# Shared expert's weights split once and reloaded as halves; routed experts' down products one step later

## The chip, the cores and the metric

The kernel runs on one core of one Trainium2 chip. The metric is the device time of one execution in microseconds, the median of several. The engines are named as in the profile: PE (TensorE, matmuls), PEld (its weight loads), DVE (VectorE), ACT (ScalarE), POOL (GpSimd) and SP (SyncE). SP and POOL issue nearly all DMAs here, each from its own queue, in program order: a DMA whose wait is not met holds back every DMA that stands behind it in that queue.

## The reference

Four sequences of 1024 tokens of width 512 go through one layer of two halves:

```python
x = x + layernorm(attention(layernorm(x)))       # lightning attention: 16 heads of 32, chunks of 128, a decayed running state
x = x + layernorm(moe(layernorm(x)))

def moe(x):                                      # 4096 tokens x 512
    shared = (silu(x @ sh_gate_w.T) * (x @ sh_up_w.T)) @ sh_down_w.T        # inner width 1408, every token
    probs = softmax(x @ router_weight.T); top 2 of 8 experts, weights divided by their sum
    for e in range(8):
        gate, up = split(x @ gate_up_proj[e].T)                             # 352 wide each
        out += (silu(gate) * up @ down_proj[e].T) * combine[:, e]
    return out + sigmoid(x @ shared_gate_w.T) * shared
```

## The kernel before

**Precision.** A large product of float32 matrices is made of three passes of a shorter type, `fp32r`: each operand is split into a high half (`_hi`, a copy rounded by ACT) and a low half (`_lo`, the rest, subtracted by DVE), and PE forms hi·hi, hi·lo and lo·hi (function `three`, lines 752 to 754). So every weight has to be split by an ACT copy and a DVE subtraction before PE can use it.

**Tiles.** The 4096 tokens are 8 blocks of 512 (`a` in the attention, `f` in the shared expert). The shared expert's inner width is 11 tiles of 128 (`NT`), so there are 88 units `n = 11 f + t`. A unit has on PE a gate product (`GA n`, 12 matmuls), an up product (`UP n`, 12) and a down product (`DN n`, 12), on ACT the silu (`SI`) and the high half of the hidden values (`HH`), on DVE the product (`SI`) and the low half (`HL`). The weights of a unit arrive as two raw pieces of 384 KB (`raw 2n` and `raw 2n+1`, issued by SP into three buffers) and are split by `SPL n half`: three ACT copies and three DVE subtractions for a unit. This is done again for each of the 8 blocks, 88 times in all. `WGU` (2) and `WDN` (3) are the numbers of buffers of gate/up and of down halves.

**Order.** `schedule()` writes one list of pieces, and every engine runs its own pieces in the order of that list. The attention pieces of a block are placed by the numbers in `PLACES` (a period of 44 for a block); the parts of the shared expert (`ffn_parts`: a first part with `GA`, a second with `UP`, a third with `DN` of the unit before) are filled in between. Attention pieces that the text speaks of: `QK` (8 products that make q and k), `V`, `S` (scores; DVE then multiplies them with the decay mask into `probsT`), `IP` (needs that `probsT`), `ST` (state), `OUT` (output product), `T1` and `T2` (transposes), `L` (residual and layernorm, about 5 us on DVE). `wa` loads one of 16 tiles of the attention weights, already stored as halves, 2 x 256 KB; `xr` loads the residual, `xin` the next block's x, `xti f` the transposed x of block `f` for the shared expert (8 loads of 256 KB, chunk by chunk, as `UP` of the last unit of block `f-1` gives the chunks free).

**The three stages.** Up to about 1200 us attention and the shared expert are interleaved (units 0 to about 58). Then the shared expert runs alone to unit 76, and in units 66 to 68 DVE works out the experts' pages of tokens (`SP 0` to `SP 5`). From about 1400 to 1890 us come the routed experts: 39 groups of 256 tokens (every fifth, from group 4 on, has only one subtile), 71 subtiles of 128 tokens, called steps `j`. Last come the 11 units of the last block with the final normalisation.

**A step of the routed experts** (`moe_step(j)`). PE: `GU j k` for k = 0 to 3 (gate and up products, 24 matmuls of 352 columns in all), `HT` (transposes of the hidden values), `XT` (transposes of the x of the next step), `MD` (down product, 9 matmuls). ACT and DVE: `WG g k` and `WD g k` split the weights of group `g` (4 and 3 pieces), `XT` and `HT` halve what PE has transposed, `MS` makes the hidden values; ACT evicts the down product (`MD`). POOL issues, in the order of the list: `rgu g` and `rdn g` (load the raw weights; there is one buffer for the down weights, so `rdn g+1` waits until DVE has split the last piece of group `g`), `xg` (gathers tokens) and `yo j` (adds the result of step j to the output in DRAM; it waits for ACT's eviction and for the adds of the group before). ACT's `WD g 0` waits for the landing of `rdn g`, and everything behind it on ACT waits with it.

Of the kernel before, what the change touches and what calls it, by code (L numbers as in the profile page):

```python
# [16 lines left out]
P = 128  # L17
D = 512
# [69 lines left out]
    "KT": (18, 27.16, 35.35, 42.69,),
    "S": (19, 20, 22.82, 23.75, 27.43, 27.98, 30.89, 30.98, 34.99, 36.49, 38.49, 39.49, 43.69, 44.69, 46.69, 47.69,),
    "V": (21.15, 21.85, 23.3, 23.85,),  # L90
    "IP": (22.07, 24.69, 29.52, 32.07, 37.88, 40.58, 46.23, 48.78,),
    "ST": (25, 32.57, 41.49, 50.17,),
    "OUT": (28.97, 35.43, 43.94, 50.69,),
    "LO": (36.6, 51,),
    "LN": (37.92, 53.57,),
    "L": (38.45, 53.31,),
    "LX": (39.15, 54.8,),
    "x1o": (39.67, 41.23, 52.1, 54.3,),
    "T2": (41.6, 42.6, 56, 56.74,),
    "xto": (58.7,),  # L100
    "R1": (58,),
    "R2": (59.41,),
    "SM1": (59.42,),
    "SM2": (60.46,),
    "SM3": (61.11,),
    "SM4": (62.32,),
    "CM": (62.12,),
    "RK": (64.43,),
    "sc": (59.36,),
    "PG": (66.47,),  # L110
# [1572 lines left out]
```

## Time and profile before

| | us |
|---|---|
| median of 3 runs | 2010.15 (2004.2 to 2010.46) |
| the profiled execution, its own time | 2009.93 |
| its span | 2008.1 |
| PE busy, of the span | 1893.5 (94%) |
| PEld busy | 1533.8 (76%) |
| DVE busy | 1197.4 (60%) |
| ACT busy | 952.2 (47%) |
| POOL busy | 434.5 (22%) |
| moved by DMA | 387.67 MB, 193 GB/s on average |

A matmul of 512 columns is shown as 0.39 us long, but the next one starts 0.23 us after it: they are pipelined, and PE's pace is read from the starts. Idle time in brackets behind a row is what the engine waited before it, and for whom. Times of rows are counted from the start of the span.

### The profile page before, as it was taken

The page shows a single profiled execution, that of the slowest core. Times are in us where ns is not written, and L with a number is a line of the kernel's source. Part 1 is how long each engine was busy: PE and PEld are TensorE (multiplying, and loading weights), DVE is VectorE, ACT ScalarE, POOL GpSimd, SP SyncE. Part 2 cuts the span into 40 slices and gives each one's busy share as a digit, 9 for nine tenths or more (in the row PEclk, how much of TensorE's full clock was granted, in tenths as well). Part 3 has the DMA queues.
Part 4 walks back from the last instruction along what each step waited for, and adds up shares of the span by engine and source line. Part 5 has one row for each costly group of instructions (what it writes and reads, how often), then busy time and mean ns, then how long its engine had stood idle before and what let it go on. Part 6 is the DMA issues. An engine that isn't in the chain of part 4 may idle for free.

```text
span 2008.1 us, 27871 instructions
## 1 busy us (share of the span) xinstructions
PE 1893.5 (94%) x9880; PEld 1533.8 (76%) x9880; DVE 1197.4 (60%) x2788; ACT 952.2 (47%) x1916; POOL 434.5 (22%) x438
## 2 busy tenths in 40 slices
PE   7779999999999999999999999999899999999997
PEld 5566777777777776777777777778899988889875
...
GB/s 304 355 266 217 67 152 219 129 144 231 67 171 211 104 118 257 123 107 206 160 115 192 142 119 152 171 227 172 187 257 253 255 253 255 251 250 253 128 280 203
DMA packets 137705, 387.67 MB, mean 193 GB/s; under 512 B 16848, under 2 KB 16992, under 8 KB 130656
## 3 DMA queue, kind: packets, MB, share of 16 engines
...
q10 hardware_dynamic: 432, 0.07, 0.0%
...
## 4 chain that ended last, share of the span: by engine, by line
PE 73%; DVE 10%; DMA 8%; ACT 4%; issue 3%; SPq 1%; POOL 1%; ACTq 0%; DVEq 0%
PE banks L752 20%; PE banks L754 20%; PE banks L753 19%; DMA moe_dn_raw<-w_dn,w_index 5%; PE banks L819 4%; PE banks L833 2%; PE banks L839 2%; PE banks L826 1%; PE banks L785 1%; DMA x<-x 1%; PE banks L940 1%; DVE probsT L1309 1%; ACT moe_dn_hi L1083 1%; PE banks L946 1%; DMA ffn_w_raw<-w_ffn 1%
## 5 line engine op out<-in xcount | busy, mean ns | idle before, releaser
L752 PE MATMUL banks<-xT_hi,ffn_gate_up_hi 128*128 128x512 f32 x704 | 298.8, 424 | 8.5 <-DMA xT_lo<-xt_scratch 5.8
L754 PE MATMUL banks<-xT_hi,ffn_gate_up_lo 128*128 128x512 f32 x704 | 277.1, 394 | 0.0
L753 PE MATMUL banks<-xT_lo,ffn_gate_up_hi 128*128 128x512 f32 x704 | 276.4, 393 | 0.0
L752 PE MATMUL banks<-moe_gu_hi,moe_xT_hi 128*128 128x352 f32 x568 | 197.4, 348 | 6.5 <-DVE moe_xT_lo L1464 6.5
L1018 ACT COPY q_one_head<-qT 32x128 f32<-32x128 f32 x512 | 151.2, 295 | 87.5 <-PE banks L819 82.3
L1457 DVE TENSOR_TENSOR moe_gu_lo<-moe_gu_raw,moe_gu_hi 128x704 fp32r<-128x704 f32 x156 | 135.9, 888 | 89.0 <-ACT moe_gu_hi L1077 88.0
L754 PE MATMUL banks<-moe_gu_hi,moe_xT_lo 128*128 128x352 f32 x568 | 184.0, 324 | 0.0
L753 PE MATMUL banks<-moe_gu_lo,moe_xT_hi 128*128 128x352 f32 x568 | 183.2, 323 | 0.0
L752 PEld LDWEIGHTS banks<-xT_hi,ffn_gate_up_hi 128*128 128x128 f32 x704 | 133.4, 189 | 52.1 <-issue 10.8
L753 PEld LDWEIGHTS banks<-xT_lo,ffn_gate_up_hi 128*128 128x128 f32 x704 | 133.6, 190 | 33.5 <-issue 9.1
L754 PEld LDWEIGHTS banks<-xT_hi,ffn_gate_up_lo 128*128 128x128 f32 x704 | 133.1, 189 | 29.1
L657 POOL DMA_INDIRECT ffn_out<-moe_y,moe_x x71 | 115.9, 1633 | 170.4 <-ACT moe_y L1103 117.3
L1440 DVE TENSOR_TENSOR ffn_gate_up_lo<-ffn_w_raw,ffn_gate_up_hi 128x768 fp32r<-128x768 f32 (+1 forms) x176 | 120.8, 686 | 43.7 <-ACT ffn_gate_up_hi L1048 43.4
L1025 ACT CAST attT_hi<-banks 128x256 fp32r<-128x256 f32 x64 | 23.7, 371 | 253.3 <-PE banks L833 253.3
...
L752 PE MATMUL banks<-ffn_down_hi,hidden_hi 128*128 128x512 f32 x308 | 133.5, 433 | 6.1 <-DVE hidden_lo L1450 6.0
L819 PE MATMUL banks<-q_one_head,kT 128*128 128x512 f32 x256 | 132.9, 612 | 1.2 <-ACT q_one_head L1018 0.6
L1461 DVE TENSOR_TENSOR moe_dn_lo<-moe_dn_raw,moe_dn_hi 128x512 fp32r<-128x512 f32 x117 | 79.4, 689 | 87.1 <-ACT moe_dn_hi L1083 86.8
L754 PE MATMUL banks<-ffn_down_hi,hidden_lo 128*128 128x512 f32 x308 | 121.7, 395 | 0.0
L753 PE MATMUL banks<-ffn_down_lo,hidden_hi 128*128 128x512 f32 x308 | 121.1, 393 | 0.0
L1077 ACT CAST moe_gu_hi<-moe_gu_raw 128x704 fp32r<-128x704 f32 x156 | 119.0, 783 | 0.0
L605 POOL DMA_INDIRECT x_normed_by_expert<-x_normed,pos_int x64 | 65.1, 1018 | 248.3 <-DVE pos_int L1409 230.1
...
## 6 DMA issues: line engine op xcount, KB each, us to landing
ffn_w_raw<-w_ffn SPq DMA_DIRECT2D x176, 384.0 KB, 3.1
...
```

Of the source, the lines that this page charges most:

```text
L605: pool.indirect_dma_start(out=xs_d[:, :], out_offset=bass.IndirectOffsetOnAxis(ap=posi[:, NC * a + c, k:k + 1], axis=0), in_=xn2[:, c, :], ...
L657: pool.indirect_dma_start(out=acc_d[:, :], out_offset=bass.IndirectOffsetOnAxis(ap=xg[:, j % XG, D + 1:DX].bitcast(I32), axis=0), in_=y[:, ...
L752: pe.matmul(out_ap, l_hi, r_hi, start=start, stop=False)
L753: pe.matmul(out_ap, l_hi, r_lo, start=False, stop=False)
L754: return pe.matmul(out_ap, l_lo, r_hi, start=False, stop=stop)
L819: mm = pe.matmul(b, kT[:, g, c * P:(c + 1) * P], qz[:, g % 2].rearrange("p h t -> p (h t)"), start=True, stop=True)
L833: mm = pe.matmul(b[r, cols], v[:, c, g * P + j * HD:g * P + (j + 1) * HD], probs[:, g % 2, j, :], start=False, stop=(gl == 1), skip_group_ ...
L1018: op = act.copy(qz[r, g % 2, j, :], qT[r, g, c * P:(c + 1) * P])
L1077: op = act.copy(gu_hi[:, i % 2, k, :], rgu[:, i % 2, k * GU:(k + 1) * GU])
L1440: op = ve.tensor_tensor(wgu_lo[:, n % WGU, gu_cut], src, wgu_hi[:, n % WGU, gu_cut].bitcast(F32), ALU.subtract)
L1457: op = ve.tensor_tensor(gu_lo[:, i % 2, k, :], rgu[:, i % 2, k * GU:(k + 1) * GU], gu_hi[:, i % 2, k, :].bitcast(F32), ALU.subtract)
L1461: op = ve.tensor_tensor(dn_lo[:, i % 2, k, :], rdn[:, k * D:(k + 1) * D], dn_hi[:, i % 2, k, :].bitcast(F32), ALU.subtract)
```

## The change

1. **Weights stored as halves.** In block 0 the weights of the shared expert are loaded raw and split as before. After each split SP stores the halves in DRAM (`wst n`: 1024 KB of gate/up, 512 KB of down). For units 11 to 76 there is no `raw` and no `SPL`; SP loads the halves instead: `wl n 0` (gate and up, 1024 KB, placed behind `UP n-2`, for whose buffer it waits) and `wl n 1` (down, 512 KB, behind `DN n-3`). Units 77 to 87, after the experts, load raw and split as before. The high and low halves of a buffer now lie side by side, so that one DMA fills both.
2. **`xti` moved.** It stands right behind `UP` of the last unit of a block, no longer ahead of the next block's first unit.
3. **A step of the routed experts in another order.** `MD` and `yo` come a step later (of step j-2, behind `GU j 0`), `XT` stands ahead of `GU j 1`, `HT` behind it.
4. **Places moved.** `PLACES` shifts as a whole by 0.07 (some by 0.03 or 0.17); `xin` comes 0.45 earlier, the first `xr` 0.71 earlier, `CM` 0.37 earlier. A few pieces change places with a neighbour through this.

```diff
 def ffn_parts(n):
...
-    if n + 1 < NF:
-        first.insert(0, ("SPL", n + 1, 0))
-        second.insert(0, ("SPL", n + 1, 1))
-        for half in range(2):
-            u = 2 * (n + 1) + half + RAW
-            if u < 2 * NF:
-                (first, second)[half].insert(1, ("raw", u))
+    for half, part in enumerate((first, second)):
+        u = 2 * (n + 1) + half + RAW
+        if u < 2 * NT or 2 * F_MOE <= u < 2 * NF:
+            part.insert(0, ("raw", u))
+        if split_here(n + 1):
+            part.insert(0, ("SPL", n + 1, half))
+    if n + 1 < NT:
+        second.insert(1, ("wst", n + 1))
     if n % F_MOE:
         third += ffn_down(n - 1)
-    if t == 0 and n != F_MOE:
-        if f:
-            first.insert(0, ("xti", f))
+    if t == NT - 1 and n + 1 < F_MOE:
+        second.append(("xti", f + 1))
+    if NT <= n + WGU < F_MOE:
+        second.append(("wl", n + WGU, 0))
+    if NT <= n + WDN - 1 < F_MOE:
+        third.append(("wl", n + WDN - 1, 1))
...
     if live:
         out += [("GU", j, 0)]
-    if j:
-        out += [("HT", j - 1)]
+    if j >= 2:
+        out += [("MD", j - 2), ("yo", j - 2)]
+        if j >= 4 and j - 4 + XG < NJ:
+            out += [("xg", j - 4 + XG)]
     split()
+    if j + 1 < NJ:
+        out += [("XT", j + 1)]
     if live:
         out += [("GU", j, 1)]
-        if j + 1 < NJ:
-            out += [("XT", j + 1)]
     split()
+    if 1 <= j <= NJ:
+        out += [("HT", j - 1)]
     if live:
         out += [("GU", j, 2), ("GU", j, 3), ("MS", j)]
-    if j:
-        out += [("MD", j - 1), ("yo", j - 1)]
-        if j >= 3 and j - 3 + XG < NJ:
-            out += [("xg", j - 3 + XG)]
...
+            elif kind == "wst":
+                n, = args
+                sp.wait_ge(v_piece, done("V", "SPL", n, 1))
+                sp.dma_start(out=wfg_d[n], in_=wgu[:, n % WGU].rearrange("p i n -> p (i n)").bitcast(F32)).then_inc(wsplit_out[n % 4], 16)
+                sp.dma_start(out=wfd_d[n], in_=wdn[:, n % WDN].rearrange("p i n -> p (i n)").bitcast(F32)).then_inc(wsplit_out[n % 4], 16)
+            elif kind == "wl":
+                n, down = args
+                ring = WDN if down else WGU
+                sp.wait_ge(*split_stored(n % NT))
+                if n - ring < NT:
+                    sp.wait_ge(*split_stored(n - ring))
+                sp.wait_ge(p_piece, done("P", "DN" if down else "UP", n - ring))
+                dst, part, landed = (wdn, wfd_d, wdn_in) if down else (wgu, wfg_d, wgu_in)
+                sp.dma_start(out=dst[:, n % ring].rearrange("p i n -> p (i n)").bitcast(F32), in_=part[n % NT]).then_inc(landed[n % ring], 16)
...
             if kind in ("GA", "UP"):
                 if kind == "GA":
-                    pe.wait_ge(v_piece, done("V", "SPL", n, 1))
+                    if split_here(n):
+                        pe.wait_ge(v_piece, done("V", "SPL", n, 1))
+                    else:
+                        pe.wait_ge(wgu_in[n % WGU], 16 * ((n - NT) // WGU + 1))
...
                 act.wait_ge(raw_in[u % RAW], 16 * (u // RAW + 1))
                 if n >= WGU:
                     act.wait_ge(p_piece, done("P", "UP", n - WGU))
+                if WGU <= n < NT:
+                    act.wait_ge(*split_stored(n - WGU))
```

SP's queue before block 2 of the shared expert, before the change. `x1` is the residual of attention block 3 (`xr 3 2` and `xr 3 3`), `ffn_w_raw` are the raw weights of units 18 to 23, `xT_hi` and `xT_lo` the first chunk of `xti 2`:

```order
L714 DMA ffn_w_raw<-w_ffn 128x768 [waits dve_piece] x9
L689 DMA x1<-x 128x512 [waits act_piece,x1_out0]
L689 DMA x1<-x 128x512 [waits act_piece,x1_out1]
L724 DMA xT_hi<-xt_scratch 128x512 [waits xT_used,xT_out]
L724 DMA xT_lo<-xt_scratch 128x512
```

The same place after it (the loads of the halves of unit 22, `xti 2`, then the halves of unit 23):

```order
L750 DMA ffn_gate_up_hi_lo<-ffn_gate_up_split 128x2048 [waits pe_piece,ffn_w_split_out0]
L750 DMA ffn_down_hi_lo<-ffn_down_split 128x1024 [waits pe_piece,ffn_w_split_out0]
L768 DMA xT_hi<-xt_scratch 128x512 [waits xT_used,xT_out]
L768 DMA xT_lo<-xt_scratch 128x512
...
L750 DMA ffn_gate_up_hi_lo<-ffn_gate_up_split 128x2048 [waits pe_piece,ffn_w_split_out1]
L750 DMA ffn_down_hi_lo<-ffn_down_split 128x1024 [waits pe_piece,ffn_w_split_out1]
L718 DMA x1<-x 128x512 [waits act_piece,x1_out0]
L718 DMA x1<-x 128x512 [waits act_piece,x1_out1]
```

The loads of x no longer stand behind the residual's, and the weights wait for PE (`pe_piece`) instead of DVE.

POOL's queue where the routed experts begin, before the change: two stores of the shared expert's last block, `rgu 3`, two more stores, `yo 0` (with the waits for those stores), `rdn 2`, `yo 1`:

```order
L616 DMA ffn_out<-shared_staged 128x512 [waits act_piece] x2
L636 DMA moe_gu_raw<-w_gu,w_index 128x2816 [waits dve_piece]
L616 DMA ffn_out<-shared_staged 128x512 [waits act_piece] x2
L657 DMA ffn_out<-moe_y,moe_x 4352x512 [waits shared_out0,shared_out1,ffn_out_zero,act_piece]
L643 DMA moe_dn_raw<-w_dn,w_index 128x1536 [waits dve_piece]
L657 DMA ffn_out<-moe_y,moe_x 4352x512 [waits act_piece]
```

The same place after it:

```order
L641 DMA ffn_out<-shared_staged 128x512 [waits act_piece] x2
L661 DMA moe_gu_raw<-w_gu,w_index 128x2816 [waits dve_piece]
L641 DMA ffn_out<-shared_staged 128x512 [waits act_piece] x2
L668 DMA moe_dn_raw<-w_dn,w_index 128x1536 [waits dve_piece]
L682 DMA ffn_out<-moe_y,moe_x 4352x512 [waits shared_out0,shared_out1,ffn_out_zero,act_piece]
L661 DMA moe_gu_raw<-w_gu,w_index 128x2816 [waits dve_piece]
```

`rdn 2` now stands ahead of `yo 0`, so that only DVE's last split of group 1 holds it.

ACT in step 20 of the routed experts (`moe_dn_hi` are the pieces `WD 11 0` to `WD 11 2`, the first of which needs the landing of `rdn 11`), before the change:

```order
L1083 CAST moe_dn_hi<-moe_dn_raw 128x512 [waits pe_piece,moe_dn_in]
L1093 CAST moe_hT_hi<-banks 128x384 [waits pe_piece]
L1083 CAST moe_dn_hi<-moe_dn_raw 128x512 [waits pe_piece,moe_dn_in]
L1088 CAST moe_xT_hi<-banks 128x512 [waits pe_piece]
L1083 CAST moe_dn_hi<-moe_dn_raw 128x512 [waits pe_piece,moe_dn_in]
L1098 ACTIVATE moe_silu<-banks 128x352 [waits dve_piece,pe_piece]
L1103 ACTIVATE moe_y<-banks,moe_x 128x512 [waits moe_y_added0,pe_piece]
```

And after it:

```order
L1134 CAST moe_dn_hi<-moe_dn_raw 128x512 [waits pe_piece,moe_dn_in]
L1154 ACTIVATE moe_y<-banks,moe_x 128x512 [waits moe_y_added1,pe_piece]
L1134 CAST moe_dn_hi<-moe_dn_raw 128x512 [waits pe_piece,moe_dn_in]
L1139 CAST moe_xT_hi<-banks 128x512 [waits pe_piece]
L1134 CAST moe_dn_hi<-moe_dn_raw 128x512 [waits pe_piece,moe_dn_in]
L1144 CAST moe_hT_hi<-banks 128x384 [waits pe_piece]
L1149 ACTIVATE moe_silu<-banks 128x352 [waits dve_piece,pe_piece]
```

`moe_hT_hi`, which PE's `MD` needs, has moved from directly behind the first of these splits to a place behind all three, and the `MD` that uses it to the step after.

## Rows read from the trace of the kernel before

**Rows 1.** The page: busy time of each engine over the span.

```profile
PE 1893.5 (94%) x9880; PEld 1533.8 (76%) x9880; DVE 1197.4 (60%) x2788; ACT 952.2 (47%) x1916; POOL 434.5 (22%) x438
```

**Rows 2.** Windows by stage: us, busy by engine, PEclk, DMA share, GB/s.

```profile
0.00:200.00 200.00, 160.12 (x785) 118.60 (x786) 106.61 (x291) 81.21 (x188) 38.11 (x57) 0.92 0.84 286
200.00:1200.00 1000.00, 969.44 (x5039) 741.86 (x5038) 593.75 (x1582) 432.14 (x958) 78.67 (x108) 1.00 0.45 152
1440.00:1890.00 450.00, 436.84 (x2588) 404.02 (x2587) 288.64 (x444) 284.52 (x509) 245.48 (x196) 1.00 0.88 245
```

**Rows 3.** Waits of PE, 200 to 1200 us: total, times, longest.

```profile
PE banks L826 <- DVE probsT L1309: 5.5, 8, 0.9
PE banks L752 <- DMA xT_lo<-xt_scratch: 3.0, 6, 1.0
PE banks L752 <- DVE probsT L1309: 2.6, 7, 0.4
```

**Rows 4.** Waits of PE, 1320 to 1890 us.

```profile
PE banks L752 <- DVE moe_hT_lo L1466: 7.9, 7, 1.7
PE banks L752 <- DVE moe_xT_lo L1464: 6.5, 3, 5.5
PE banks L946 <- DVE moe_hidden L1470: 4.6, 5, 1.2
```

**Rows 5.** Groups by line: what splits the shared expert's weights.

```profile
L1440 DVE TENSOR_TENSOR ffn_gate_up_lo<-ffn_w_raw,ffn_gate_up_hi 128x768 fp32r<-128x768 f32 (+1 forms) x176 | 120.8, 686 | 43.7 <-ACT ffn_gate_up_hi L1048 43.4
L1437 DVE TENSOR_TENSOR ffn_down_lo<-ffn_w_raw,ffn_down_hi 128x512 fp32r<-128x512 f32 x88 | 60.6, 688 | 38.1 <-ACT ffn_down_hi L1046 36.7
```

**Rows 6.** Timeline of PE before and at `GA 22`: start, length, form, idle before.

```profile
549.77 0.39 PE L753 MATMUL banks<-xT_lo,ffn_gate_up_hi 128*128 128x512 f32 x1
550.00 0.39 PE L754 MATMUL banks<-xT_hi,ffn_gate_up_lo 128*128 128x512 f32 x1
...
559.59 1.02 PE L819 MATMUL banks<-q_one_head,kT 128*128 128x512 f32 x2
...
564.90 0.49 PE L752 MATMUL banks<-xT_hi,ffn_gate_up_hi 128*128 128x512 f32 x1 [0.35 <-DMA xT_lo<-xt_scratch]
```

**Rows 7.** Timeline of SP, 549 to 562 us.

```profile
552.74 0.85 SPq L689 DMA_DIRECT2D x<-x  x2
553.68 0.39 SPq L724 DMA_DIRECT2D xT_hi<-xt_scratch  x1
```

**Rows 8.** DVE on the raw shared weights, 1292 to 1317 us; then PE at `DN 66`.

```profile
1292.00:1317.00 25.00, 2.92 (x4) 0.93 0.48 152
...
1317.27 0.51 PE L752 MATMUL banks<-ffn_down_hi,hidden_hi 128*128 128x512 f32 x1 [4.11 <-DVE hidden_lo L1450]
```

**Rows 9.** Timeline of DVE, POOL and ACT, 1412 to 1429 us.

```profile
1412.44 0.69 DVE L1461 TENSOR_TENSOR moe_dn_lo<-moe_dn_raw,moe_dn_hi 128x512 fp32r<-128x512 f32 x1 [2.28 <-ACT moe_dn_hi L1083]
...
1420.37 1.51 POOL L643 DMA_INDIRECT moe_dn_raw<-w_dn,w_index  x1 [0.30 <-DVE moe_gu_lo L1457]
...
1428.04 0.62 ACT L1083 CAST moe_dn_hi<-moe_dn_raw 128x512 fp32r<-128x512 f32 x1 [7.72 <-DMA moe_dn_raw<-w_dn,w_index]
```

**Rows 10.** Windows, 1427.5 to 1434.4 us; columns as in Rows 2.

```profile
1427.50:1434.40 6.90, 4.32 (x16) 4.20 (x17) 3.93 (x7) 4.22 (x8) 2.91 (x3) 0.51 0.74 231
```

**Rows 11.** Timeline of POOL, 1536 to 1546 us, and of ACT and PE there.

```profile
1538.39 0.94 POOL L643 DMA_INDIRECT moe_dn_raw<-w_dn,w_index  x1 [0.30 <-DVE moe_gu_lo L1457]
...
1544.79 0.62 ACT L1083 CAST moe_dn_hi<-moe_dn_raw 128x512 fp32r<-128x512 f32 x1 [2.54 <-DMA moe_dn_raw<-w_dn,w_index]
...
1546.66 0.50 PE L752 MATMUL banks<-moe_dn_hi,moe_hT_hi 128*128 128x512 f32 x1 [1.18 <-DVE moe_hT_lo L1466]
```

**Rows 12.** DMA issues, whole span: count, KB each, median us to landing.

```profile
ffn_w_raw<-w_ffn SPq DMA_DIRECT2D x176, 384.0 KB, 3.1
xt_scratch<-xT_staged_lo POOLq DMA_DIRECT2D x7, 1024.0 KB, 8.2
```

**Rows 13.** The loads that touch `att_w_lo`, 200 to 1200 us.

```profile
DMA to landing us min/median/max: 2.8/4.5/9.1
```

More of the change, by code:

```diff
@@ L88 @@
[L88 to L110, printed above, removed]
+    "N1": (3.48, 4.07, 5.52, 6.52,),
+    "T1": (5.62, 6.95, 7.62, 8.62,),
+    "wa": (7.25, 7.43, 7.61, 7.79, 10.52, 10.08, 12.52, 13.52, 14.17, 15.52, 16.52, 18.84, 23.22, 23.37, 23.52, 23.27,),
+    "QK": (9.66, 11.07, 12.07, 13.22, 14.07, 15.07, 16.07, 16.78,),
+    "xr": (23.12, 24.37, 44.52, 44.74,),
@@ new lines @@
+    "Z": (16.39, 18.62, 20.77, 21.47, 25.5, 26.5, 28.65, 29.05, 33.66, 33.97, 36.82, 37.52, 42.06, 43.54, 44.99, 45.76,),
+    "KT": (18.17, 27.23, 35.38, 42.76,),
+    "S": (19.17, 20.07, 22.99, 23.92, 27.5, 28.05, 30.96, 31.05, 35.02, 36.52, 38.52, 39.52, 43.76, 44.76, 46.76, 47.76,),
+    "V": (21.22, 21.92, 23.37, 23.92,),
+    "IP": (22.24, 24.86, 29.59, 32.14, 37.91, 40.61, 46.3, 48.85,),
+    "ST": (25.17, 32.64, 41.52, 50.24,),
+    "OUT": (29.14, 35.5, 43.97, 50.76,),
+    "LO": (36.67, 51.07,),
@@ L111 @@
+    "LN": (37.99, 53.64,),
+    "L": (38.52, 53.38,),
+    "LX": (39.22, 54.87,),
+    "x1o": (39.74, 41.3, 52.17, 54.37,),
+    "T2": (41.67, 42.67, 56.07, 56.81,),
+    "xto": (58.77,),
+    "R1": (58.07,),
+    "R2": (59.48,),
+    "SM1": (59.49,),
+    "SM2": (60.53,),
+    "SM3": (61.18,),
+    "SM4": (62.39,),
+    "CM": (61.75,),
+    "RK": (64.5,),
+    "sc": (59.43,),
+    "PG": (66.54,),
     "W": (),
@@ L149, in attention_offsets, with split_here, raw_turn, raw_unit @@
     return s
+def split_here(n):
+    return n < NT or F_MOE <= n < NF
+def raw_turn(u):
+    return u if u < 2 * NT else u - 2 * (F_MOE - NT)
+def raw_unit(turn):
+    return turn if turn < 2 * NT else turn + 2 * (F_MOE - NT)
 def ffn_parts(n):
@@ L303, in schedule @@
     cut = ends.index(("EV", BEFORE - 1, 2))
-    start, tail = moe_step(0), moe_step(NJ)
+    start = moe_step(0)
     seq += ends[:2] + start[:1] + ends[2:cut] + [("xti", BEFORE)] + start[1:] + ends[cut:]
@@ L308, in schedule @@
     after = [part for n in range(F_MOE, NF) for part in ffn_parts(n)]
-    seq += tail[:1] + after[0] + tail[1:]
+    seq += moe_step(NJ) + after[0] + moe_step(NJ + 1)
     after[0] = []
@@ L418, in build @@
         raw = sb("ffn_w_raw", [RAW, UNIT])
-        wgu_hi = sb("ffn_gate_up_hi", [WGU, 2 * D], F32R)
-        wgu_lo = sb("ffn_gate_up_lo", [WGU, 2 * D], F32R)
-        wdn_hi = sb("ffn_down_hi", [WDN, D], F32R)
-        wdn_lo = sb("ffn_down_lo", [WDN, D], F32R)
+        wgu = sb("ffn_gate_up_hi_lo", [WGU, 2, 2 * D], F32R)
+        wdn = sb("ffn_down_hi_lo", [WDN, 2, D], F32R)
+        wgu_hi, wgu_lo = (wgu[:, :, i, :] for i in range(2))
+        wdn_hi, wdn_lo = (wdn[:, :, i, :] for i in range(2))
         shs = sb("shared_staged", [2, D])
@@ L555, in build @@
         sh_out = [sem(f"shared_out{i}") for i in range(2)]
+        wsplit_out = [sem(f"ffn_w_split_out{i}") for i in range(4)]
+        wgu_in = [sem(f"ffn_gate_up_in{i}") for i in range(WGU)]
+        wdn_in = [sem(f"ffn_down_in{i}") for i in range(WDN)]
         raw_in = [sem(f"raw_in{i}") for i in range(RAW)]
@@ L712, in sp_piece @@
                 else:
-                    sp.wait_ge(v_piece, done("V", "SPL", *divmod(u - RAW, 2)))
-                sp.dma_start(out=raw[:, u % RAW, :], in_=w_ffn[u // 2 % NT, u % 2]).then_inc(raw_in[u % RAW], 16)
+                    sp.wait_ge(v_piece, done("V", "SPL", *divmod(raw_unit(i - RAW), 2)))
+                sp.dma_start(out=raw[:, i % RAW, :], in_=w_ffn[u // 2 % NT, u % 2]).then_inc(raw_in[i % RAW], 16)
             elif kind == "xti":
@@ L899, in pe_ffn @@
                 pe.wait_ge(v_piece, done("V", "HL", n))
+                if not split_here(n):
+                    pe.wait_ge(wdn_in[n % WDN], 16 * ((n - NT) // WDN + 1))
                 if n == F_MOE:
@@ L1037, in act_ffn @@
                 half, = args
-                u = 2 * n + half
+                u = raw_turn(2 * n + half)
                 act.wait_ge(raw_in[u % RAW], 16 * (u // RAW + 1))
@@ L1432, in dve_ffn @@
                 half, = args
-                src = raw[:, (2 * n + half) % RAW, :]
+                src = raw[:, raw_turn(2 * n + half) % RAW, :]
                 ve.wait_ge(a_piece, done("A", kind, n, half))
```

14 lines of the change are left out of this document (7 added, 7 removed), and 2 rows, old and new, of the table PARTS.

## The prediction

> **What bounds the kernel now.** I read the page first, then the windows by stage, then the waits of PE in each stage, and last the timeline around the waits that stand out. PE is busy for 1893.5 us of 2008.1 [rows 1], no other engine for more than 60% except PE's own weight loads. The number of matmuls is not touched by the change, so its worth can only be PE's waits, some 115 us at most, and the lowered clock that follows long ones. By stage [rows 2]: the opening (to 200 us) leaves 40 us idle with the DMA engines 84% busy; the interleaved stage leaves 31 us of 1000; the routed experts, 1440 to 1890 us, leave 13 of 450. The reader is to see in the windows how thin PE's losses are spread: a gain has to be collected from many small places, and each must be a place that this change touches.
>
> **The splits that go.** DVE spends 120.8 + 60.6 us on 88 units [rows 5], 2.06 us each; 66 units lose them, 136 us of DVE work, and ACT loses the three copies ahead of them. Almost all of it lies beside PE's matmuls and is worth nothing by itself. It is worth something where PE waits for a DVE result that stands behind a split. In the interleaved stage PE waits for `probsT` in two rows, 5.5 + 2.6 us in 15 waits [rows 3]. Some of these are behind `L`, which stays, some behind a split. Evictions of banks that DVE does late are not all in these rows. Bounds: 0, if DVE's queue is held by what stays, and 13 us, if the 8.1 us go and as much again as half of that in the unlisted ones. I take 6, nearer the middle, because the waits are many and short and a split is 0.4 to 0.95 us long.
>
> **DVE's chain in the page stage.** From 1292 to 1317 us DVE works nearly without a pause on the pages, and `DN 66` starts at 1317.27 after 4.11 us of waiting for `hidden_lo`. Four subtractions of raw shared weights stand in that stretch, 2.92 us together [rows 8], and they go. PE gets just that, since DVE sets this place; whatever PE saves a few us earlier (its x for block 6 arrives sooner too) is waited for here. Gain 2.9; bounds 0, if ACT's evictions ahead of `HH 66` set it next, and 4.1, the whole wait.
>
> **`xti` earlier.** `GA 22` waits chunk by chunk. The last of its four chunks starts at 564.90. At the pace of undisturbed matmuls, 550.00 - 549.77 = 0.23, it would start 11 matmuls (two of scores, nine of `GA`) after 559.59, at 562.1 [rows 6]: 2.8 us lost, of which I leave 0.3 to the start of another product. SP issues the residual's loads at 552.74 and only then the first of xT at 553.68 [rows 7], though `UP 21` was running at 549.77 and gave the first chunk free within its first three matmuls. Now `xti 2` stands ahead of the residual and, for block 3, ahead of all that it followed. `GA 33` loses the same. PE's recorded waits for these are 3.0 us in 6 [rows 3]; the rest is loads landing between matmuls. Gain 5, bounds 3 and 6.
>
> **Start of the routed experts.** `rdn 2` was issued at 1420.37 behind `yo 0`; ACT took its data at 1428.04 after 7.72 us idle [rows 9], `XT 4` stood behind that, and PE waited 5.5 us [rows 4]. Then the granted clock was 0.51 for 6.9 us [rows 10]; PE worked 4.3 us in it, at half pace, which costs another 2.2. In the new order `rdn 2` needs only DVE's last split of group 1, which runs at 1412.44 for 0.69 [rows 9], so the data lands 1413.1 + (1428.04 - 1420.37) = 1420.8, before PE asks for `GU 4 0`. Gain 7, of 7.7; bounds 3 (it is slower, behind `rgu 3` in the queue) and 7.7.
>
> **Routed experts, steady.** PE waits 7.9 us for `moe_hT_lo` and 4.6 us for `moe_hidden`, 12 waits [rows 4]. One of them: `rdn 11` is issued at 1538.39 behind a `yo` and an `xg`; ACT takes it at 1544.79 after 2.54 us; the high half of hT stands behind, and PE's `MD` starts 1.18 us late, at 1546.66 [rows 11]. Now `HT` has three quarters of a step and `MD` a step more, `rdn` stands ahead of the `yo` that held it in this place, and between ACT's stall and PE's need lie GU products of about 1.1 us each. What is late next: `XT`, also behind the splits on ACT, for which PE leaves two GU, one `HT` and one GU, 3.5 us, where it had 4.3 (`MD` was among them). Halving takes 1.5, so ACT may be 2 us late before PE sees it, and it was 2.54 late here. Gain 10 of 12.5; bounds 3 and 12.5. The DMAs of `yo` only shift.
>
> **What it adds.** 66 units load 1536 KB for 768: 52 MB more, and 11 stores of 1536 KB, 17 MB. Nothing in the trace is a 1024 KB load on SP; the nearest rows are 1024 KB stores with 8.2 us to landing for the second of two, and 3.1 us for 384 KB [rows 12]. Even 8.2 is hidden: from `UP n-2` to `GA n` PE has at least `DN`, `GA`, `UP`, `DN`, 48 matmuls of 0.23 or 11 us. `wl` waits for PE, so SP can run less far ahead; but between the release of each attention tile and its use stands the same PE work as before, at least 24 matmuls and three transposes, some 6.7 us (tile 0 of a block); for tile 11 it is 7.6, for tile 4 8.2. Those loads take 4.5 us in the middle and 9.1 at most [rows 13]. The 16 engines are 45% busy in this stage at 152 GB/s [rows 2]; 69 MB more over some 1150 us is 60 GB/s more, which makes it some 63%. Cost: none, if the median holds; if tiles 0, 4 and 11 of six blocks all took 9.1 us, 2.4 + 0.9 + 1.5 = 4.8 us a block, 29 us. I take 3, near the median. The Trainium skill, page "DMA: Bandwidth & Descriptors", section "Issuing engines are not separate DMA queues", says that DMAs of all issuers run on the same 16 engines and interleave; by that the stores and loads would slow the attention's loads and POOL's too, and the sum would move toward the 29 us. No row here shows the added load; the trace's own 9.1 us agrees that loads in a crowd take twice as long.
>
> The stores add a wait on ACT (`SPL n` for the store of `n-2`), which holds copies and with them PE. The tightest is unit 2: between the end of split 0 and split 2 lie about `GA 0` and `UP 0`, 24 matmuls or 5.5 us, and a store of 1024 KB may take 8.2 [rows 12], 2.7 us more. I take 0, for a store alone in its queue lands sooner, and 3 us either way for the opening, the places moved included; their swaps of neighbours change nothing else that I can price.
>
> **Sum.** 6 + 2.9 + 5 + 7 + 10 = 30.9, less 3, is 28 us. The profiled execution took 2009.9 (span 2008.1 and 1.8 around it), the median of the runs is 2010.15; so 2010 - 28 = **1982 us**. All upper bounds: 13 + 4 + 6 + 7.7 + 12.5 + 3 = 46, 1964. All lower ones without the traffic: 0 + 0 + 3 + 3 + 3 = 9, 2001.
>
> **Rivals.**
> - *The waits among the experts move on to `XT` and the `yo` queue.* Their DMA engines are 88% busy [rows 2], so the landing of `rdn` is set by traffic, not by its place; ACT is as late as before and now holds `XT`. For it: slack of `XT` shrinks by 0.8 us. Against it: POOL was what delayed `rdn` in [rows 11]. The experts then give 3 + 2 instead of 17: 28 - 12 = 16 us, 1994.
> - *DVE and ACT work was hidden anyway and the traffic takes the rest.* The interleaved stage gives 0 instead of 6 and the traffic takes 20 instead of 3: 28 - 23 = 5 us, 2005; with all 29 of it, 2014. For it: the splits' waits are short ones; against it: no unit of the load is late by the count of PE work above.
> - *Slower: the attention's weights come late.* Place: `QK 0`, `QK 4` and `V 0` of each block. It decides once their landing passes 6.7 us; every us beyond costs up to 3 x 6 = 18 us. At 9.1 us it costs 29 instead of 3, which leaves 2 of the gain, 2008; two us beyond that another 36, which makes 2044. For it: the traffic of this stage grows by 40%. Against it: only one `wl` at a time is in flight and those tiles are issued after attention products, when the last `wl` has mostly landed.
>
> **How the numbers follow.** The forecast case, 15 to 44 us faster, 0.70; the first rival 0.14; the second 0.08; slower 0.06; better than all bounds 0.02. A measurement of this kernel tells 0.3% (6 us) from no change. Faster: 0.70 + 0.14 + 0.02 = 0.86; within, 0.08; slower, 0.06. The range takes the first two cases, 1965 to 2001, and leaves 0.16 out.
>
> **What would show it.** In the changed profile: `ffn_w_raw` about 44 loads instead of 176 and DVE about 1060 us busy; no wait for `xT_lo` at blocks 2 and 3; `DN 66` still waiting for DVE; no half clock where the experts begin; waits for `moe_hT_lo` and `moe_hidden` gone and at most 3 us for `moe_xT_lo`; the stage 200 to 1200 shorter by some 8 us with DMA at about 0.6. I am wrong if PE waits for `att_w`, `ffn_gate_up_hi_lo` or a store, or if the expert stage is not shorter by 10 us or more.

## The result and the profile after

The changed kernel takes 1996.7 us (median of 16 runs, 1985.8 to 2004.3) against 2008.1 us for the kernel before (16 runs, 2004.1 to 2013.8). The ratio is 0.9941, with a 95% interval of 0.993 to 0.9952: 0.6% or 11 us faster, inside the range, but not half of the 28 us forecast. The profiled execution took 2002.2 us, its span 2000.4, so the two profiles differ by 7.7 us, and the account below is of these.

Between the starts of certain pieces on PE (first matmul of each, from PE's timeline) the two profiled executions took, in us:

| stretch on PE | before | after | gained | forecast |
|---|---|---|---|---|
| start to `GA 2` | 196.7 | 193.3 | 3.4 | 0 |
| `GA 2` to `GA 55` | 998.2 | 996.9 | 1.3 | 8 (6 + 5 - 3) |
| `GA 55` to `GU 0 0` | 200.8 | 196.2 | 4.6 | 2.9 |
| `GU 0 0` to `GU 5 0` | 43.1 | 33.2 | 9.9 | 7 |
| `GU 5 0` to `GU 70 0` | 452.8 | 461.8 | -9.0 | 10 |
| `GU 70 0` to `UP 87` | 95.9 | 98.4 | -2.5 | 0 |

The forecast fails in two rows: the interleaved stage, and above all the routed experts, where a gain of 10 became a loss of 9. The stretch to `GU 0 0` gained more than its upper bound of 4.1.

The page of the changed kernel, busy time [rows 1]:

```profile
PE 1895.7 (95%) x9880; PEld 1536.0 (77%) x9880; DVE 1083.5 (54%) x2590; ACT 844.6 (42%) x1718; POOL 439.6 (22%) x438
```

DVE has lost 114 us and ACT 108, PE's work is the same. The windows by stage [rows 2, 10]:

```profile
0.00:200.00 200.00, 163.24 (x808) 120.82 (x812) 107.32 (x292) 81.12 (x188) 38.10 (x57) 0.93 0.88 311
200.00:1200.00 1000.00, 971.82 (x5043) 744.92 (x5036) 513.62 (x1445) 361.51 (x822) 78.94 (x109) 0.99 0.56 201
1400.00:1440.00 40.00, 39.91 (x238) 36.77 (x236) 24.41 (x38) 24.27 (x44) 17.02 (x14) 1.00 0.75 220
1440.00:1890.00 450.00, 433.60 (x2529) 398.92 (x2530) 282.72 (x431) 272.56 (x493) 247.43 (x191) 0.99 0.84 239
```

Where the experts begin (1400 to 1440) PE is busy throughout at full clock; the half clock of [rows 10] is gone. After it, PE is busy for 3 us less than before. PE's waits from 200 to 1200 us [rows 3]:

```profile
PE banks L796 <- DMA att_w_lo<-att_w_split: 6.7, 1, 6.7
...
PE banks L796 <- DVE probsT L1360: 2.3, 7, 0.3
PE banks L870 <- DVE probsT L1360: 2.1, 7, 0.9
```

The waits for `probsT` fell from 8.1 to 4.4 us and those for `xT_lo` are gone, as forecast; in their place stands one wait that is new. The waits among the experts, 1320 to 1880 us [rows 4]:

```profile
PE banks L796 <- DVE moe_hT_lo L1517: 12.5, 7, 2.9
PE banks L796 <- DVE moe_xT_lo L1515: 4.1, 6, 1.2
```

`moe_hidden` and the 5.5 us for `moe_xT_lo` are gone; `moe_hT_lo` has grown from 7.9 to 12.5 us in the same number of waits. Both new losses, seen close. First SP and PE around `QK 5 6`, timeline:

```profile
748.58 0.38 SPq L768 DMA_DIRECT2D xT_hi<-xt_scratch  x1
...
753.34 0.59 SPq L768 DMA_DIRECT2D xT_lo<-xt_scratch  x1
754.03 0.67 SPq L750 DMA_DIRECT2D ffn_gate_up_hi_lo<-ffn_gate_up_split  x1
754.75 0.66 SPq L731 DMA_DIRECT2D att_w_hi<-att_w_split  x1
755.44 0.49 SPq L731 DMA_DIRECT2D att_w_lo<-att_w_split  x1
...
769.51 0.77 PE L796 MATMUL banks<-x_normedT_hi,att_w_hi 128*128 128x512 f32 x1 [6.69 <-DMA att_w_lo<-att_w_split]
```

The weights of `QK 5 6` (`wa 5 6`) are issued behind the eight loads of `xti 3` and the 1024 KB of `wl 34 0`, and land 14 us later. PE then waits 6.69 us and starts its next matmuls 0.43 us apart instead of 0.23: the granted clock has fallen to half (1.2 GHz) within that wait, at 764.8 us, and stays there for 10 us. The windows of this place and of the first of three such places among the experts:

```profile
764.80:775.00 10.20, 5.49 (x13) 4.36 (x14) 3.08 (x18) 0.00 (x0) 0.00 (x0) 0.50 0.63 239
1495.00:1499.00 4.00, 4.00 (x16) 3.35 (x15) 0.90 (x3) 1.63 (x3) 1.60 (x2) 0.57 0.86 317
```

Second, step 23 of the experts, timeline of POOL, ACT and PE:

```profile
1547.15 1.62 POOL L682 DMA_INDIRECT ffn_out<-moe_y,moe_x  x1 [3.01 <-ACT moe_y L1154]
1549.08 1.23 POOL L646 DMA_INDIRECT moe_x<-x_normed_by_expert,x_index  x1 [0.30 <-issue]
1550.61 1.34 POOL L668 DMA_INDIRECT moe_dn_raw<-w_dn,w_index  x1 [0.30 <-DVE moe_hidden L1521]
...
1556.76 0.62 ACT L1134 CAST moe_dn_hi<-moe_dn_raw 128x512 fp32r<-128x512 f32 x1 [2.54 <-DMA moe_dn_raw<-w_dn,w_index]
1557.28 0.47 ACT L1144 CAST moe_hT_hi<-banks 128x384 fp32r<-128x384 f32 x1
...
1558.62 0.50 PE L796 MATMUL banks<-moe_dn_hi,moe_hT_hi 128*128 128x512 f32 x1 [1.66 <-DVE moe_hT_lo L1517]
```

`rdn 13` stands behind `yo 20`, which waited 3.01 us for ACT's eviction, and an `xg`; it lands 6.1 us after its issue, ACT stops 2.54 us for it, `HT 22` stands right behind that stop, and `MD 22` starts 1.66 us late. This repeats at `MD 13`, 22, 31, 40, 49 and 58, once in nine steps. The 9.0 us are accounted for by the window of the whole stretch in each kernel (before, then after):

```profile
1438.80:1891.60 452.80, 439.64 (x2602) 406.47 (x2601) 289.17 (x445) 285.65 (x510) 245.49 (x196) 1.00 0.87 244
```

```profile
1419.60:1881.40 461.80, 445.31 (x2603) 409.81 (x2602) 293.65 (x447) 282.82 (x510) 256.39 (x198) 0.99 0.84 241
```

Of the 9.0 us, 461.8 - 445.3 = 16.5 against 13.2, so 3.3, are more idle time, and 5.7 are matmuls that took longer, nearly all of it in the three periods of half clock.

### The profile page after: what moved, and what is told of

It is laid out like the page before. It is cut to its first block, busy times and chain, and to the rows that moved or that the text cites. A ratio compares the mean times of both kernels' runs of the same rounds, so it can differ in the third digit from the quotient of the medians.

```text
span 2000.4 us, 27565 instructions
## 1 busy us (share of the span) xinstructions
PE 1895.7 (95%) x9880; PEld 1536.0 (77%) x9880; DVE 1083.5 (54%) x2590; ACT 844.6 (42%) x1718; POOL 439.6 (22%) x438
## 4 chain that ended last, share of the span: by engine, by line
PE 56%; DMA 5%; DVE 5%; ACT 2%; issue 1%; POOL 1%; SPq 1%; ACTq 0%; DVEq 0%
PE banks L796 16%; PE banks L798 16%; PE banks L797 16%; DMA moe_dn_raw<-w_dn,w_index 3%; PE banks L863 2%; PE banks L989 1%; DMA ffn_w_raw<-w_ffn 1%; PE banks L877 1%; PE banks L995 1%; PE banks L883 1%; PE banks L870 1%; DMA att_w_lo<-att_w_split 1%; PE banks L829 1%; ACT moe_dn_hi L1134 0%; DVE fin_stats L1535 0%
## 5 line engine op out<-in xcount | busy, mean ns | idle before, releaser
L796 PE MATMUL banks<-xT_hi,ffn_gate_up_hi_lo 128*128 128x512 f32 x704 | 296.7, 422 | 9.8 <-DMA xT_lo<-xt_scratch 3.3
L798 PE MATMUL banks<-xT_hi,ffn_gate_up_hi_lo 128*128 128x512 f32 x704 | 276.8, 393 | 0.0
L797 PE MATMUL banks<-xT_lo,ffn_gate_up_hi_lo 128*128 128x512 f32 x704 | 276.1, 392 | 0.0
L796 PEld LDWEIGHTS banks<-xT_hi,ffn_gate_up_hi_lo 128*128 128x128 f32 x704 | 133.1, 189 | 49.2 <-issue 10.2
L797 PEld LDWEIGHTS banks<-xT_lo,ffn_gate_up_hi_lo 128*128 128x128 f32 x704 | 133.2, 189 | 33.9 <-issue 8.9
L798 PEld LDWEIGHTS banks<-xT_hi,ffn_gate_up_hi_lo 128*128 128x128 f32 x704 | 132.9, 189 | 29.0
L682 POOL DMA_INDIRECT ffn_out<-moe_y,moe_x x71 | 120.7, 1699 | 143.0 <-ACT moe_y L1154 63.1
L796 PE MATMUL banks<-ffn_down_hi_lo,hidden_hi 128*128 128x512 f32 x308 | 131.2, 426 | 2.3 <-DVE hidden_lo L1501 2.3
L1498 DVE TENSOR_TENSOR hidden<-banks,hidden 128x512 f32<-128x512 f32 x77 | 53.2, 691 | 129.2 <-PE banks L798 100.3
L796 PE MATMUL banks<-x_normedT_hi,att_w_hi 128*128 128x512 f32 x256 | 106.5, 416 | 17.6 <-DVE x_normedT_lo L1339 6.9
L1360 DVE TENSOR_TENSOR probsT<-banks,decay_mask 128x512 f32<-128x512 f32 x128 | 88.1, 689 | 63.7 <-PE banks L863 61.1
L798 PE MATMUL banks<-ffn_down_hi_lo,hidden_lo 128*128 128x512 f32 x308 | 120.8, 392 | 0.0
L797 PE MATMUL banks<-ffn_down_hi_lo,hidden_hi 128*128 128x512 f32 x308 | 120.2, 390 | 0.0
```

Of the source, the lines that this page charges most:

```text
L682: pool.indirect_dma_start(out=acc_d[:, :], out_offset=bass.IndirectOffsetOnAxis(ap=xg[:, j % XG, D + 1:DX].bitcast(I32), axis=0), in_=y[:, ...
L796: pe.matmul(out_ap, l_hi, r_hi, start=start, stop=False)
L797: pe.matmul(out_ap, l_hi, r_lo, start=False, stop=False)
L798: return pe.matmul(out_ap, l_lo, r_hi, start=False, stop=stop)
L1360: op = ve.tensor_tensor(probs[:, g % 2, :, :], chunked(b), mask[:, GH * g:GH * (g + 1), :], ALU.mult)
L1498: op = ve.tensor_tensor(hid[:, :], up_ps, sg[:, :], ALU.mult)
```

## The experiments

Twelve kernels, each timed against the kernel before and looked at in one profile. They were timed in three lots: experiment 1 and the first kernels of 2 and 3; the second kernels of 2 and 3 and the first of 4 and 6; the rest. The kernel before had medians of 2009.7, 2016.1 and 2009.1 us in them, so kernels of different lots are compared by their ratios. `GU 5 0` to `GU 70 0` is called the expert stretch.

**1. The old order of a step in the changed kernel, and the new order alone.** Two theories: A, the new order loses the 9 us; B, the halves' traffic or something earlier does.

```diff
     if live:
         out += [("GU", j, 0)]
-    if j >= 2:
-        out += [("MD", j - 2), ("yo", j - 2)]
...
+    if j:
+        out += [("HT", j - 1)]
     split()
-    if j + 1 < NJ:
-        out += [("XT", j + 1)]
     if live:
         out += [("GU", j, 1)]
+        if j + 1 < NJ:
+            out += [("XT", j + 1)]
     split()
-    if 1 <= j <= NJ:
-        out += [("HT", j - 1)]
     if live:
         out += [("GU", j, 2), ("GU", j, 3), ("MS", j)]
+    if j:
+        out += [("MD", j - 1), ("yo", j - 1)]
```

That is the first kernel's edit; the second makes the same edit the other way round in the kernel before.

> The changed kernel with the old order of an expert step (MD of the last step at its end, HT behind GU 0, rdn as before); all else as changed. Theory A (the new order itself costs the experts time): from GU 5 to GU 70 the old 453 us come back instead of 462, no half clock in that stage, MD's waits for moe_hT_lo no longer than 1.8 us; the 5.5 us wait where the experts begin comes back too, with its half clock, some 7 to 9 us. Total within 4 us of the changed kernel, 1993 to 2001. Rival B (the experts are slower for another reason: the weights' halves and their traffic, or the clock after the earlier stages): that stretch stays at 460 or more and the total is 2003 or more.

> The kernel before with only the new order of an expert step. Theory A: GU 5 to GU 70 takes 460 to 463 us instead of 453, with waits of MD for moe_hT_lo of 1.5 to 3 us and periods of half clock; the wait at GU 4 0 is gone (7 to 9 us won), so the total is within 4 us of the kernel before. Rival B: the stretch takes 443 to 453 us as it was forecast, and the total is 8 to 17 us below the kernel before.

Measured: 1995.6 us, ratio 0.993 (0.9911 to 0.9949), and 2009.5 us, ratio 0.9997 (0.9982 to 1.0012). The expert stretch of the first, then of the second, with PE's waits in it:

```profile
1426.40:1877.40 451.00, 439.65 (x2601) 406.62 (x2600) 288.92 (x445) 285.75 (x510) 246.45 (x196) 1.00 0.87 245
...
PE banks L796 <- DVE moe_hT_lo L1517: 8.0, 7, 1.7
PE banks L995 <- DVE moe_hidden L1521: 3.1, 5, 0.9
```

```profile
1429.40:1891.90 462.50, 446.98 (x2602) 411.17 (x2601) 293.68 (x447) 283.02 (x510) 259.73 (x198) 0.99 0.84 241
...
PE banks L752 <- DVE moe_hT_lo L1466: 12.8, 7, 3.3
```

Theory A holds and B falls: 462 us go with the new order in both surroundings, 451 to 453 with the old. With the new order alone the gain at the start (`GU 0 0` to `GU 5 0` 33.2 instead of 43.1) is just eaten by the stretch behind it.

**2. What the attention's weights wait for.** One kernel puts `xti 3` and `wl 34 0` behind `wa 5 7` in the list (`moved` takes pieces out and puts them behind another), one puts every `xti` back.

```diff
-PIECES = schedule()
+PIECES = moved(schedule(), [("xti", 3), ("wl", 34, 0)], ("wa", 5, 7))
```

```diff
-    if t == NT - 1 and n + 1 < F_MOE:
-        second.append(("xti", f + 1))
+    if t == 0 and f and n != F_MOE:
+        first.insert(0, ("xti", f))
```

> The changed kernel with xti 3 and wl 34 0 behind wa 5 7 in the queue of SP, so that the weights of QK 5 6 no longer stand behind 3 MB of other loads. Theory C (that queue place caused the 6.7 us wait of QK 5 6 and the half clock behind it): no wait for att_w_lo over 1 us, no half clock at 765 us, GA 33 is reached 5 to 8 us earlier than in the changed kernel, total 1989 to 1992 against its 1997. Rival D (the wait is the traffic's, or xT takes its place): the same time at GA 33 within 2 us, with a new wait for att_w or for xT_lo of 3 us or more, total 1995 to 1998.

> The changed kernel with xti back at its old place (ahead of the first unit of a block, so xti 3 behind xin 6 and xti 2 behind the residual's loads; now behind the 1.5 MB of wl 23 too). Theory C (the 6.7 us wait at QK 5 6 comes from xti's new place, not from the added traffic): no wait for att_w_lo over 1 us and no half clock at 765 us, but waits for xT_lo at GA 22 and GA 33 come back with 3 us or more each, so GA 34 within 3 us of the changed kernel. Rival D (the added traffic is what makes att_w late): a wait for att_w_lo of 3 us or more remains in block 5. Total 1993 to 2000 for C, 2000 or more for D.

Measured: 1993.8 us, ratio 0.9919 (0.9896 to 0.9941), and 2038.9 us, ratio 1.0116 (1.0093 to 1.0139). The medians alone don't tell the first from the changed kernel; its profile does: `GA 33` starts at 782.0 us instead of 787.5, with no half clock ahead of it, and 5.6 us remain at `GA 55`. The wait for the weights, 560 to 800 us, is 2.5 us at `V 5 0`, whose load now stands behind the same 3 MB:

```profile
PE banks L803 <- DMA att_w_lo<-att_w_split: 2.5, 1, 2.5
```

So theory C: the place in the queue made the wait, though 2.5 us of it came back elsewhere, where C allowed 1. The other kernel agrees (no wait for `att_w_lo` at all) and shows something that neither theory had: by the ratios it is 1.8% or 35 us slower than the changed kernel, where C said 4 us at most. `GA 2` to `GA 55` takes 1026.2 us instead of 996.9. PE's waits from 200 to 1250 us:

```profile
PE banks L796 <- DMA xT_lo<-xt_scratch: 23.7, 11, 4.5
```

At the old place `xti` now also stands behind the 1.5 MB of the next unit's halves. With weights as halves the early `xti` is not an extra of 5 us but a condition.

**3. The same buffer, other neighbours.** Two kernels move what stands around ACT's stop for `moe_dn_raw`: the first puts `yo` and `xg` behind the first split of a step, the second puts `HT` ahead of it.

```diff
-        out += [("MD", j - 2), ("yo", j - 2)]
-        if j >= 4 and j - 4 + XG < NJ:
-            out += [("xg", j - 4 + XG)]
+        out += [("MD", j - 2)]
     split()
+    if j >= 2:
+        out += [("yo", j - 2)]
+        if j >= 4 and j - 4 + XG < NJ:
+            out += [("xg", j - 4 + XG)]
```

```diff
             out += [("xg", j - 4 + XG)]
+    if 1 <= j <= NJ:
+        out += [("HT", j - 1)]
     split()
...
-    if 1 <= j <= NJ:
-        out += [("HT", j - 1)]
```

> The changed kernel with yo and xg of a step behind its first split, so that where that split is the last of a group's down weights rdn goes out ahead of yo and xg (rdn 13 ahead of yo 20). Theory E (ACT stops at WD g 0 because rdn stands behind a yo that waits for ACT's eviction, one step later than before, and HT stands behind that stop): ACT's waits for moe_dn_raw fall below 25 us from 41, MD's waits for moe_hT_lo from 12.5 to 6 us or less, GU 5 to GU 70 from 462 to 448 to 455 us, total 1985 to 1991. Rival F (the landing of rdn is set by the traffic of the queue, or the stop is only moved): that stretch stays within 3 us of 462 and the total within 3 us of the changed kernel.

> The changed kernel with HT of a step ahead of the first split, right behind MD, so that four GU products and XT lie between HT and its MD on PE instead of three GU products (and HT stands ahead of all splits of its step on ACT). Theory J (the new order gave the chain from HT to MD no more room than the old one, three GU products in both, and that is why MD waits): waits for moe_hT_lo fall from 12.5 us to under 2, those for moe_xT_lo stay at 4, GU 5 to GU 70 in 448 to 453 us, total 1984 to 1989. Rival K (ACT's stop for moe_dn_raw hits XT instead): moe_xT_lo or moe_hidden takes 8 us or more, that stretch 457 to 463, total 1993 to 1998.

Measured: 1997.5 us, ratio 0.9942 (0.9925 to 0.996), expert stretch 459.3; and 1994.5 us, ratio 0.9907 (0.9877 to 0.9936), expert stretch 458.4. PE's waits in the stretch, of the one and of the other:

```profile
PE banks L798 <- DVE moe_xT_lo L1517: 12.0, 14, 2.2
PE banks L798 <- DVE moe_hT_lo L1519: 1.9, 3, 1.1
```

```profile
PE banks L796 <- DVE moe_xT_lo L1515: 10.9, 10, 2.5
PE banks L995 <- DVE moe_hidden L1521: 5.2, 5, 1.9
```

Both of my theories fall. The waits for `moe_hT_lo` go as meant, and the same microseconds come back as waits for `moe_xT_lo`. ACT's stops even grew with `rdn` ahead of `yo`, from 41.1 us in 19 to 55.9 in 26. With one buffer the order chooses who is late, and how long (451 to 462 us for the stretch); no order tried gets below 451.

**4. Two buffers for the raw down weights.** In the changed kernel, and in the kernel before with nothing else.

```diff
-        rdn = sb("moe_dn_raw", [DT * D], scope=phase2)
+        rdn = sb("moe_dn_raw", [2, DT * D], scope=phase2)
...
-            if kind == "WD" and n == DT - 1 and g + 1 < NG:
-                out.append(("rdn", g + 1))
+            if kind == "WD" and n == DT - 1 and g + 2 < NG:
+                out.append(("rdn", g + 2))
```

> The changed kernel with two buffers for the raw down weights, each loaded a group earlier (rdn g+2 behind the split of group g); the order of the step is the changed one. Theory H (all losses of the stage start where ACT stops for moe_dn_raw, because its one buffer is loaded 6 to 7 us behind the last split): ACT's waits for moe_dn_raw fall from 41 us to under 5, PE's waits for moe_hT_lo and moe_xT_lo from 16 to under 4, no half clock, GU 5 to GU 70 in 440 to 446 us instead of 462, total 1976 to 1983. Rival I (another wait takes over: moe_gu_raw, moe_x or the engines of the DMA, 88% busy): ACT waits for moe_gu_raw or PE for the banks instead, that stretch 455 or more, total 1990 or more.

> The kernel before with two buffers for the raw down weights and nothing else. Theory H says that the single buffer set all losses of the experts in either order: GU 5 to GU 70 falls from 453 to 436 to 439 us and GU 3 to GU 5 from 21 to 14, so the kernel is 20 to 25 us faster than before (1.0 to 1.2%), more than the whole change gave. Rival L (the two buffers help only the new order, and the old one keeps its short waits for moe_hidden and moe_hT_lo): that stretch stays at 446 or more and the kernel gains 12 us or less.

Measured: 1980.2 us, ratio 0.982 (0.9804 to 0.9836), and 1982.6 us, ratio 0.9883 (0.9869 to 0.9898). The expert stretch of the first, then of the second:

```profile
1421.80:1858.20 436.40, 436.40 (x2603) 406.84 (x2602) 295.28 (x447) 282.54 (x510) 254.83 (x197) 1.00 0.87 254
```

```profile
1425.40:1861.00 435.60, 435.60 (x2602) 407.64 (x2601) 286.48 (x445) 285.80 (x510) 244.16 (x198) 1.00 0.90 255
```

PE is busy in every microsecond of it, at full clock, in either order, with the DMA engines as busy as before (0.87 and 0.90). Theory H holds, and one buffer more makes the kernel before 1.2% or 24 us faster by the ratio (27 by the medians, 2009.1 to 1982.6), over twice what the change gave: 17 us in the stretch, and 8 at the start (`GU 0 0` to `GU 5 0` 35.3 instead of 43.1). The Trainium skill, page "Trainium Kernel Development and Optimization", section "Best Practices", has double buffering as a general rule; here the runs agree, with 452.8 against 435.6 us.

**5. More traffic.** Both repairs (the two buffers, and `xti 3` behind `wa 5 7`), and both with a copy in DRAM behind each load of gate and up halves. The copies' data isn't used.

```diff
+                if not down:
+                    sp.dma_start(out=more_d[n], in_=wfg_d[n % NT]).then_inc(more, 16)
```

> The changed kernel with both repairs: two buffers for the raw down weights, and xti 3 with wl 34 0 behind wa 5 7. If the two add up: GU 5 to GU 70 in 436 to 438 us, GA 33 reached 5 to 6 us earlier than with the two buffers alone, total 1974 to 1977. If they don't (a later stage takes back what the earlier gains): 1979 or more.

> The kernel of both repairs with a copy of 1024 KB from DRAM to DRAM behind each load of a unit's gate and up halves: 66 copies, 69 MB read and 69 MB written on top, about twice what the change itself added in that stage. If the added traffic was hidden, as the forecast has it (3 us of cost), GA 2 to GA 55 grows by 6 us or less against the kernel without the copies and att_w is waited for less than 3 us. If traffic is what ate the gain, it grows by 15 us or more, with waits for att_w_lo and xT_lo.

Measured: 1970.2 us, ratio 0.9807 (0.9795 to 0.982), and 2010.0 us, ratio 1.0004 (0.9993 to 1.0015). One of six executions of the first took 6877.8 us, which nothing here explains; the others lie between 1967.5 and 1972.1. The repairs add up. `GA 2` to `GA 55` takes 988.7 us in it and 1023.0 with the copies, 34 us more. The kernel with the copies, 200 to 1200 us, its windows, its wait for the weights, and their landing:

```profile
200.00:1200.00 1000.00, 956.35 (x4907) 732.97 (x4902) 504.51 (x1430) 355.03 (x807) 78.42 (x108) 0.98 0.66 242
...
PE banks L808 <- DMA att_w_lo<-att_w_split: 16.3, 5, 5.4
...
DMA to landing us min/median/max: 2.8/5.3/15.2
```

Against the same kernel without the copies the median landing hardly moves (5.0 us, 5.3 here; 4.5 in [rows 13]); the longest goes from 10.2 to 15.2 (9.1 in [rows 13]), and those are what PE waits for. The DMA engines are 66% busy, 57% without the copies. The mean share says little about the load that is late. The Trainium skill, page "DMA: Bandwidth & Descriptors", section "Issuing engines are not separate DMA queues", says that all DMAs share the same engines, whoever issues them. For the attention's weights this run doesn't separate the queue from the engines behind it, since the copies stand ahead of them in SP's own queue. But POOL's queue agrees with the page: its two 1024 KB stores of the transposed x land in 4.7 and 8.2 us (median) in the kernel before, 7.6 and 10.2 in the changed one, and 8.8 and 11.4 with the copies, though only SP's traffic grew.

**6. The old order with the repairs.** With one buffer and `yo 0` behind `rdn 2`, and with two buffers.

Both have the edit of the first kernel of experiment 1 and that of the first of experiment 2; one adds the line below, the other the edit of experiment 4.

```diff
+PIECES = moved(PIECES, [('yo', 0)], ('rdn', 2))
```

> The changed kernel with the old order of an expert step, yo 0 put behind rdn 2 in POOL's queue, and xti 3 with wl 34 0 behind wa 5 7 on SP: it keeps what gained and undoes what lost. If the gain at the start of the experts comes from POOL's queue alone, GU 3 to GU 5 takes 14 us as in the changed kernel (19 with the old step alone), GU 5 to GU 70 takes 451 as with the old step, GA 33 is 6 us earlier: total 1983 to 1987. Rival G (rdn 2 is late in the old order for another reason, such as ACT's order, or the gains don't add up): GU 3 to GU 5 stays at 18 to 21 us, total 1988 to 1993.

> Both repairs with the old order of an expert step. With two buffers ACT never stops for moe_dn_raw, so the order should hardly matter: GU 5 to GU 70 in 436 to 440 us, GU 70 to UP 77 in 11.4 us instead of 13.5 (the last down products don't stand behind the last group), total 1972 to 1976. If the old order has waits of its own (moe_hidden behind GU 0, one product after the hidden values are made), that stretch is 442 or more and the total 1978 or more.

Measured: 1989.7 us, ratio 0.987 (0.985 to 0.9889), and 1968.1 us, ratio 0.9803 (0.9791 to 0.9816): the fastest of all, 2% under the kernel before, though not to be told from the 0.9807 with the new order. With one buffer `GU 0 0` to `GU 5 0` takes 35.3 us (40.9 without the move of `yo 0`, 33.2 in the changed kernel) and the expert stretch 451.2. So the gain at the start was POOL's queue, but for 2.1 us. Two buffers and the old order, expert stretch:

```profile
1414.10:1849.70 435.60, 435.60 (x2602) 407.65 (x2601) 286.58 (x445) 285.81 (x510) 245.02 (x197) 1.00 0.89 254
```

## Why the prediction was right in direction and wrong in size

**Routed experts, steady: the step that failed.** The term of 10 us rested on "`HT` has three quarters of a step and `MD` a step more", and on `rdn` standing ahead of the `yo` that held it. The first gives no room. In the list `MD` comes one product later, not a step (behind `GU 0` of the next step instead of at the end of its own), and so does `HT`. Between `HT` and its `MD` PE has three GU products in the new order (`GU` 2 and 3, `GU` 0 of the next step), and had three and an `XT` in the old one.

The second holds where I had read it, and not everywhere. In 18 of the groups `rdn` leaves POOL 0.27 us behind DVE's last split, where it left 1.7 to 2.8 us behind it, and PE's old waits at `MD 10`, 19, 28 and so on are gone. But `rdn 13`, and every fifth from `rdn 8` on, still stands behind a `yo`. It is no later than it was: POOL issues it 2.57 us behind the last split in both kernels, and ACT stopped for it before, too, 3.25 us against 2.54 now. What changed is that `HT 22` stood ahead of that stop. The same place in the kernel before, POOL and ACT:

```profile
1562.52 0.94 POOL L643 DMA_INDIRECT moe_dn_raw<-w_dn,w_index  x1 [0.30 <-issue]
...
1564.39 0.47 ACT L1093 CAST moe_hT_hi<-banks 128x384 fp32r<-128x384 f32 x1
...
1569.28 0.62 ACT L1083 CAST moe_dn_hi<-moe_dn_raw 128x512 fp32r<-128x512 f32 x1 [3.25 <-DMA moe_dn_raw<-w_dn,w_index]
```

So ACT's stops became fewer while PE's waits became longer. ACT's waits among the experts, before and after:

```profile
ACT moe_dn_hi L1083 <- DMA moe_dn_raw<-w_dn,w_index: 63.4, 30, 3.4
```

```profile
ACT moe_dn_hi L1134 <- DMA moe_dn_raw<-w_dn,w_index: 41.1, 19, 3.8
```

The cause of the stops, one buffer whose next load leaves only behind the last split and lands some 6.6 us later, I had named in a row and not priced: the forecast moved the neighbours of ACT's stop, and it was the stop that had to go. Measured -9 for +10; two buffers give 16 to 17 over the old order. How the 9 us divide stays open. The load before, `rdn 12`, is later than it was (3.42 us behind the last split instead of 0.27), and `HT` stands behind the stop; taking `rdn` out from behind `yo`, or `HT` out from behind the stop, gave back 2.5 and 3.4 us (experiment 3).

**The first rival** came nearest in time (1994) and in its effect, waits that move on. Its reason was wrong: with two buffers the DMA engines are as busy, and PE waits for nothing.

**`xti` earlier, cost of the traffic.** The early `xti` won 1.9 us at `GA 22` (to `GA 23` 11.2 us, before 13.1) and the same at `GA 33`, 3.8 of the 5, and the waits for `probsT` fell by 3.7 us. What lacked was the price of `xti` for those behind it: I counted the time that PE leaves each attention tile, and not the 3 MB that stand ahead of one of them in SP's queue. That is one wait of 6.7 us, and half clock behind it, in which 5.5 us of PE's work cost another 2.7; the repair gets 5.6 us of this back by `GA 55`, for `V 5 0` then waits. With it mended, `GA 2` to `GA 55` gains 7.4 us (990.8), and in the three other kernels that have the repair and no copies 9.5, 7.5 and 6.4, where the sum had 8. What lies beyond the 3.8 can't be told apart: no run undoes the splits, the traffic or the moved places alone. The third rival named this wait, its limit of 6.7 us of landing and the wrong tiles. The added traffic slowed POOL's large stores (experiment 5), but cost nothing that shows in these sums; it has no room left, though, since 138 MB more cost 34 us.

**The page stage and the start of the experts** were right in their mechanism. `DN 66` still waits for DVE, 1.73 us instead of 4.11 [rows 8]. The stretch gained 4.6 us, though, where 2.9 were forecast and 4.1 was the bound: before the change 3.5 us of half clock followed the wait at `DN 66` (granted clock 0.51 from 1318.3 to 1321.8 us), and they are gone; the forecast had no term for the clock there. The wait at `GU 4 0` went through POOL's queue. Of the 9.9 us at the start, 2.1 are one down product (nine matmuls) that the new order puts off: it comes back behind the experts, where `GU 70 0` to `UP 77` takes 13.5 us, and 11.4 with the old order.

**The opening** gained 3.4 us in this pair of profiles, but that isn't shown to be the change: three profiles with the old places reach `GA 2` at 191.7, 196.0 and 196.7 us, eleven with the new ones between 192.8 and 195.1. Zero, give or take 3, stands.
